# The final norms of a decoder layer: two blocks in one chain, a last accumulation in halves, stores of a quarter megabyte

## The reference

```python
x = _layernorm(x + _L0_ffn_ref(x, gate_weight, gate_up_proj, down_proj, layer_alpha))
# _layernorm: (x - mean) / sqrt(var + 1e-5) over the 256 features
# expert_step, 32 times: h = silu(x @ Wg.T) * (x @ Wu.T); acc += (h @ Wd.T) * c_e[:, None]
```

## Time and profile before

| | |
|---|---|
| device time, 3 runs | 897.95, 898.0, 899.88 us, median 898.0 |
| the profiled execution | 901.3 us, its span 899.5 us, so 1.8 us lie around the span |
| busy: PE, DVE, ACT, POOL | 848.8, 635.6, 281.1, 126.5 us |
| chain that ended last | PE 83%, DVE 11%, issue 3%, ACT 2% |
| last 39.5 us (from 860): PE, DVE, ACT, POOL busy | 26.9, 27.4, 13.0, 7.8 us |
| last instruction of an engine ends, end of the span | 896.4, 899.5 us |

### The profile page before, as it was taken

How to read it: one execution, slowest core, us unless ns; L and a number is a source line. 1 busy time by engine, 2 the same in 40 slices (tenths; PEclk the granted TensorE clock), 3 DMA queues, 4 the chain that set the end, 5 groups by cost and what they waited for, 6 DMA issues and landing times.

```text
span 899.5 us, 14653 instructions
## 1 busy us (share of the span) xinstructions
PE 848.8 (94%) x5696; PEld 668.4 (74%) x5696; DVE 635.6 (71%) x1390; ACT 281.1 (31%) x502; POOL 126.5 (14%) x101
## 2 busy tenths in 40 slices
PE   5999999999999999999797999999999999999994
PEld 4967677776777768776566788888888888888873
DVE  3565787878878888779687866656665666666557
ACT  4521153112432124211354423233332323232232
POOL 2014400343013330134122100000000000000021
PEclk9999999999999999999998999999999999999997
DMA  9210000100001000000310041020302020000001
GB/s 346 107 36 2 1 2 1 32 17 17 1 1 48 1 16 1 0 25 4 128 58 24 1 140 52 22 65 1 111 23 65 0 86 36 23 1 1 1 23 71
DMA packets 12686, 35.84 MB, mean 40 GB/s; under 512 B 1488, under 2 KB 2384, under 8 KB 12112
## 3 DMA queue, kind: packets, MB, share of 16 engines
q1 hardware_dynamic: 12624, 34.98, 11.1%
HBM read 30.33 MB, written 2.36 MB: 36 GB/s over the span
## 4 chain that ended last, share of the span: by engine, by line
PE 83%; DVE 11%; issue 3%; ACT 2%; DMA 0%; POOL 0%; ACTq 0%; DVEq 0%
PE ps L243 21%; PE ps L244 20%; PE ps L245 20%; PE ps L1398 6%; PE ps L1478 4%; PE ps L1469 2%; PE ps L1280 2%; PE ps L1454 1%; PE ps L1316 1%; PE ps L1234 1%; DVE small L255 1%; DVE small L1079 1%; PE ps L1445 1%; PE ps L1345 1%; DVE stats L923 1%
## 5 line engine op out<-in xcount | busy, mean ns | idle before, releaser
L500 DVE TENSOR_TENSOR su<-sg,ps 128x512 f32<-128x512 f32 x96 | 66.0, 688 | 134.4 <-PE ps L245 133.2
L243 PE MATMUL ps<-y_hi,f_hi 128*128 128x512 f32 x384 | 150.6, 392 | 0.0
L244 PE MATMUL ps<-y_lo,f_hi 128*128 128x512 f32 x384 | 150.1, 391 | 0.0
L245 PE MATMUL ps<-y_hi,f_lo 128*128 128x512 f32 x384 | 150.1, 391 | 0.0
L370 ACT ACTIVATE sg<-ps 128x512 f32<-128x512 f32 x96 | 57.4, 598 | 264.4 <-PE ps L245 264.4
L723 POOL TENSOR_TENSOR roped<-prod 128x512 f32<-128x512 f32 x64 | 81.0, 1288 | 175.3 <-DVE prod L1024 175.3
L1024 DVE TENSOR_TENSOR prod<-ps,ropeq 128x512 f32<-128x512 f32 x128 | 79.3, 681 | 27.9 <-PE ps L245 27.3
L245 PEld LDWEIGHTS ps<-y_hi,f_lo 128*128 128x128 f32 x384 | 72.5, 189 | 15.3
L243 PEld LDWEIGHTS ps<-y_hi,f_hi 128*128 128x128 f32 x384 | 72.5, 189 | 14.9
L244 PEld LDWEIGHTS ps<-y_lo,f_hi 128*128 128x128 f32 x384 | 72.4, 189 | 15.0
L243 PE MATMUL ps<-xT_hi,a_hi 128*128 128x512 f32 x192 | 78.8, 410 | 2.1 <-DVE xT_lo L949 2.1
(11 more groups left out here) (157 smaller groups left out, 1369.5 us busy)
## 6 DMA issues: line engine op xcount, KB each, us to landing
cb<-routing SPq DMA_DIRECT2D x32, 256.0 KB
f_raw<-in_L_ffn_gate_up_proj SPq DMA_DIRECT2D x8, 768.0 KB, 5.2
f_raw<-in_L_ffn_down_proj SPq DMA_DIRECT2D x8, 384.0 KB, 5.8
xb<-in_x SPq DMA_DIRECT2D x4, 512.0 KB, 4.2
lq<-in_L_xattn_Wq SPq DMA_DIRECT2D x1, 2048.0 KB, 14.4
x2T_all<-in_L_xattn_Wo SPq DMA_DIRECT2D x1, 2048.0 KB, 8.3
x2T_all<-x2T SPq DMA_DIRECT2D x4, 512.0 KB, 3.2
out<-res SPq DMA_DIRECT2D x4, 512.0 KB, 2.6
```

What stands on the lines that cost most here:

```text
L243: pe.matmul(dst, l_hi, r_hi, start=first, stop=False, skip_group_check=check)
L244: pe.matmul(dst, l_hi, r_lo, start=False, stop=False, skip_group_check=check)
L245: return pe.matmul(dst, l_lo, r_hi, start=False, stop=last, skip_group_check=check)
L500: dve.tensor_tensor(su[:, k % 2], sg[:, k % 2], bank(2 * (k % 2) + 1), ALU.mult).then_inc(s_su, 1)
```

## The change

The ends of blocks 0 and 1 are placed by tables, one for each part: turn_out at the end of steps 17 and 20, stats at the end of steps 18 and 21, scale at the end of steps 19 and 22, and apply at the head of steps 20 and 23, ahead of the Silu. Accumulate(7) is two instructions, one for each half of the features; turn_out takes the features' half as its outer loop, and for block 3 the second half alone waits for the second instruction. Stats(2) and stats(3) are followed by one scale chain over 8 columns (8 bn_aggr, then the 12 tiny instructions on 128x8). Of blocks 2 and 3 VectorE applies tiles 0 and 1, ScalarE tiles 2 and 3. Their results leave in four stores of 256 KB, one for each pair of tiles.

```diff
-    FINAL_STEP = 18
+    TURN_OUT_STEPS, STATS_STEPS, SCALE_STEPS, APPLY_STEPS = (17, 20), (18, 21), (19, 22), (20, 23)
 # ScalarE
             for k in range(STEPS):
+                if last and k in APPLY_STEPS:
+                    final_apply(APPLY_STEPS.index(k))
                 act.wait_ge(s_g, base + k + 1)
 ...
-                if last and k == FINAL_STEP + 3:
-                    final_apply(0)
             if last:
                 hi(STEPS - 1)
-                final_apply(1)
                 final_apply(2)
                 final_apply(3)
         def final_apply(n):
-            act.wait_ge(s_scale, n + 1)
-            for t in range(2 if n == LAST else TILES):
+            act.wait_ge(s_scale, min(n, LAST - 1) + 1)
+            for t in range(0 if n < LAST - 1 else 2, TILES):
 # SyncE
+        for n in range(LAST - 1):
+            sp.wait_ge(s_res, TILES * (n + 1))
             sp.dma_start(out[n], res[:, n]).then_inc(s_out, 16)
+        for n in (LAST - 1, LAST):
+            sp.wait_ge(s_res_end, 2 * (n - LAST + 2))
+            sp.dma_start(out[n, :, 0:2], res[:, n, 0:2]).then_inc(s_out, 16)
+            sp.wait_ge(s_res, TILES * (LAST - 1) + 2 * (n - LAST + 2))
+            sp.dma_start(out[n, :, 2:4], res[:, n, 2:4]).then_inc(s_out, 16)
 # VectorE
+        def final_stats(n):
+            y = final_sum(n)
+            own.need()
+            for t in range(TILES):
+                dve.wait_ge(s_ft, n + 1 + (t // 2 if n == LAST else 0))
+                own.step(dve.bn_stats(fst[:, TILES * n + t, :], y[:, t]))
+        def final_scale(n, blocks):
+            i = slice(TILES * n, TILES * (n + blocks))
 ...
-                dve.tensor_tensor(acc[:, :, cols(n)], acc[:, :, cols(n)], ps[:, 6:8, :], ALU.add).then_inc(s_acc, 1)
+                for m in (slice(0, KC),) if nb < NB - 1 or not last else (slice(0, 1), slice(1, 2)):
+                    dve.tensor_tensor(acc[:, m, cols(n)], acc[:, m, cols(n)], ps[:, 6 + m.start:6 + m.stop, :], ALU.add)\
+                        .then_inc(s_acc, 1)
 ...
+                if last and k in STATS_STEPS:
+                    final_stats(STATS_STEPS.index(k))
+                if last and k in SCALE_STEPS:
+                    final_scale(SCALE_STEPS.index(k), 1)
             if last:
-                final_norm(1, 1)
-                final_norm(2, 0)
+                final_stats(LAST - 1)
                 accumulate(NB - 1)
-                final_norm(2, 1)
-                final_norm(3, 0)
-                final_norm(3, 1)
+                final_stats(LAST)
+                final_scale(LAST - 1, 2)
 ...
 # TensorE, turn_out and its places
+                for m in range(KC):
+                    if n == LAST and m == 1:
+                        pe.wait_ge(s_acc, GROUPS * BLOCKS + 2)
+                    for t in range(TILES):
 ...
-                if last and k == FINAL_STEP:
-                    turn_out(0)
-                if last and k == FINAL_STEP + 3:
-                    turn_out(1)
+                if last and k in TURN_OUT_STEPS:
+                    turn_out(TURN_OUT_STEPS.index(k))
```

More of the change, by code:

```diff
@@ L147, in build @@
     res = sb(ffn, "res", [P, BLOCKS, TILES, D])
[L148 to L152, removed]
+    fst = sb(ffn, "fst", [P, BLOCKS * TILES, 6])
+    fmv = sb(ffn, "fmv", [P, BLOCKS * TILES, 2])
+    fnt = sb(ffn, "fnt", [P, 2, BLOCKS * TILES])
+    fscale = sb(ffn, "fscale", [P, 2, BLOCKS * TILES])
     ffn.close()
@@ L403, in final_apply @@
             y = final_sum(n)
-            act.wait_ge(s_scale, n + 1)
-            for t in range(2 if n == LAST else TILES):
-                act.activation(res[:, n, t], y[:, t], ACT.Identity, bias=fscale[:, n, 1, t:t + 1],
-                               scale=fscale[:, n, 0, t:t + 1]).then_inc(s_res, 1)
+            act.wait_ge(s_scale, min(n, LAST - 1) + 1)
+            for t in range(0 if n < LAST - 1 else 2, TILES):
+                i = TILES * n + t
+                act.activation(res[:, n, t], y[:, t], ACT.Identity, bias=fscale[:, 1, i:i + 1],
+                               scale=fscale[:, 0, i:i + 1]).then_inc(s_res, 1)
         over_groups(act, body)
@@ L450, in ffn_sync @@
                     load_c(w, 2 * it + w + 2, n)
[L451 to L454, removed]
+        for n in range(LAST - 1):
+            sp.wait_ge(s_res, TILES * (n + 1))
             sp.dma_start(out[n], res[:, n]).then_inc(s_out, 16)
-        sp.wait_ge(s_out, 16 * BLOCKS)
+        for n in (LAST - 1, LAST):
[3 more added lines that the diff above has]
+            sp.dma_start(out[n, :, 2:4], res[:, n, 2:4]).then_inc(s_out, 16)
@@ L458, in ffn_vector @@
+        sp.wait_ge(s_out, 16 * (BLOCKS + 2))
     def ffn_vector(dve, own, shift_logits, route):
         dve.sem_inc(s_acc, 1)
-        def final_norm(n, part):
+        def final_stats(n):
             y = final_sum(n)
             own.need()
[L465 to L478, removed]
+            for t in range(TILES):
+                dve.wait_ge(s_ft, n + 1 + (t // 2 if n == LAST else 0))
+                own.step(dve.bn_stats(fst[:, TILES * n + t, :], y[:, t]))
@@ new lines, in final_scale @@
+        def final_scale(n, blocks):
+            i = slice(TILES * n, TILES * (n + blocks))
+            own.need()
+            for t in range(i.start, i.stop):
+                own.step(dve.bn_aggr(fmv[:, t, :], fst[:, t, :]))
+            own.need()
+            own.step(dve.tensor_scalar(fnt[:, 0, i], fmv[:, i, 1], LN_EPS, None, ALU.add))
+            rsqrt(dve, own, fnt[:, 0, i], fscale[:, 0, i], fnt[:, 1, i])
+            own.need()
+            dve.scalar_tensor_tensor(out=fscale[:, 1, i], in0=fmv[:, i, 0], scalar=-1.0, in1=fscale[:, 0, i],
+                                     op0=ALU.mult, op1=ALU.mult).then_inc(s_scale, 1)
+            dve.wait_ge(s_scale, n + 1)
@@ L516, in body @@
                     route(LAST, ROUTE_STEPS.index(k))
[L517 to L520, removed]
+                if last and k in STATS_STEPS:
+                    final_stats(STATS_STEPS.index(k))
+                if last and k in SCALE_STEPS:
+                    final_scale(SCALE_STEPS.index(k), 1)
             if last:
-                final_norm(1, 1)
-                final_norm(2, 0)
+                final_stats(LAST - 1)
                 accumulate(NB - 1)
-                final_norm(2, 1)
-                final_norm(3, 0)
-                final_norm(3, 1)
[L528 to L531, removed]
+                final_stats(LAST)
+                final_scale(LAST - 1, 2)
+                for n in (LAST - 1, LAST):
+                    y = final_sum(n)
+                    for t in (0, 1):
+                        i = TILES * n + t
+                        dve.tensor_scalar(res[:, n, t], y[:, t], fmv[:, i, 0:1], fscale[:, 0, i:i + 1],
+                                          ALU.subtract, ALU.mult).then_inc(s_res_end, 1)
         over_groups(dve, body)
@@ L579, in turn_out @@
                 f = FINAL_BANKS[n]
-                for t in range(TILES):
-                    for m in range(KC):
+                for m in range(KC):
+                    if n == LAST and m == 1:
+                        pe.wait_ge(s_acc, GROUPS * BLOCKS + 2)
+                    for t in range(TILES):
                         c = n * BT + t * P
@@ L584, in turn_out @@
                                           acc[:, m, c:c + P], ident[:])
-                mm.then_inc(s_ft, 1)
+                        if m == KC - 1 and (t == TILES - 1 or n == LAST and t == 1):
+                            mm.then_inc(s_ft, 1)
             for k in range(STEPS):
```

## The result

The changed kernel is slower: median 902.68 us of 21 runs (900.51 to 904.21) against 899.73 of 21 runs of the kernel before on the same chips. The ratio is 1.0036 (95% interval 1.0026 to 1.0046), that is 3.2 us (2.3 to 4.1). Forecast were 3.6, put on 898.0, the median of three runs: 901.6. The median of the 21 runs before is 1.7 higher than that, which is why 902.68 lies above 901.6 although the change cost less than forecast. The profiled execution has a span of 902.2 us, before 899.5.

What follows compares the result with a forecast made beforehand. TensorE was taken to bound the kernel until the last steps, VectorE the end behind dn(23). Later end including stores 2.8 plus clock 0.8 gave 3.6 us slower, 901.6 us on the median 898.0; range 899.2 to 904.0.

Steps and rivals of the forecast that it cites:

- The clock: TensorE's clock around dn(22) and dn(23), after two waits of 1.8 us: may fall; 0.8 us taken, bounds 0 and 2.7.
- Accumulate(5) behind scale(0): Step 20: accumulate(5) and dn(18) 1.44 us later, turn_out(1)'s 0.68 wait gone; TensorE 0.76 later from up(22).
- Accumulate(6): Step 23: scale(1) ahead of it makes it 2.20 us later; TensorE waits 1.8 us before dn(21).
- Apply(1) ahead of Silu(23): Step 23, ScalarE: holds Silu(23), Copy(22), rest(22); second TensorE wait 1.8 us, dn(22) 4.0 later, dn(23) 4.3 later.
- The tail: Behind dn(23): from the last dn on the end is 1.7 us shorter; last apply 2.6 later than before.
- the rival with columns priced one by one: Shared scale chain: tiny instructions on 8 columns cost 12 x 0.16 = 1.9 us more, 903.5; chance 0.03.
- The stores: End of the kernel: a megabyte leaves in about a microsecond; last landing 2.4 to 3.0 us later, 2.8 taken.
- the first rival, the clock that holds: Clock holds or bytes are quick: only 2.4 to 3.0 us slower, 900.4 to 901.0; chance 0.2.
- The rival *faster: Silu(23) and Copy(22) not held: only step 20's 0.76 reaches dn(23), the shorter end wins, 897.1; chance 0.09.

Runs made afterwards that it cites:

- apply_behind: Changed kernel with apply(0) and apply(1) at the end of steps 20 and 23, behind Silu and Copy; ratio 1.0059 to the kernel before.
- apply1_last: Changed kernel with apply(1) moved behind the loop, apply(0) still ahead of Silu(20); ratio 1.0027 to the kernel before.
- loop_only: Kernel before with only the change's placement of turn_out, stats, scale and apply, old tail kept; ratio 1.0039 to the kernel before.
- block2_early: one_more_step with turn_out(2) between up(23) and dn(21), block 2's own scale chain ahead of accumulate(7), block 2 stored whole; ratio 0.9947 to the kernel before.
- loop_back: Changed kernel with blocks 0 and 1 placed as in the kernel before, new tail kept; ratio 0.9998 to the kernel before.
- one_more_step: Changed kernel with stats at the end of steps 17 and 20, scale 18 and 21, apply 19 and 23 behind Silu and Copy; ratio 0.9969 to the kernel before.
- acc_whole: Changed kernel with accumulate(7) as one 128x1024 instruction, all 8 transposes behind it; ratio 1.0038 to the kernel before.

## Why the prediction was right

The mechanism held point by point. The clock's term didn't, and two errors of the end cancelled.

- *Accumulate(5) behind scale(0)*: its start was predicted at 866.48 and is found at 866.56, dn(18)'s second matmul at 868.13 and 868.24. Turn_out(1) has no wait, as said, and up(22) is 0.8 us later than before (0.76 predicted).
- *Accumulate(6)*: predicted at 881.62 and found at 881.65; dn(21)'s second matmul at 883.27 and 883.33.
- *Apply(1) ahead of Silu(23)*: the Silu was predicted at 883.57 and is found at 883.47, rest(22) is ready at 885.93 (predicted 886.06). TensorE's second wait is there and ends with it, hc(23) is 1.6 us long under GpSimd, and dn(23)'s second matmul is at 888.89 (predicted 889.03).
- *The tail*: predicted 1.7 us shorter from the last dn to the last apply's end, found 10.78 - 8.79 = 2.0. Stats(3) begin 2.3 us behind the last matmul's start where 2.5 were estimated, and the longer chain costs less: 8 bn_aggr take 0.64 us where four took 0.37, 0.27 more and not 0.4. The 12 tiny instructions take 0.17 each on 8 columns, against 0.16 on 4, so the rival with columns priced one by one falls.
- *The stores*: the sum gives them 2.8 - 2.6 = 0.2 us more than before; they take 0.5 more (3.6 against 3.1 us behind the last apply). This hides the 0.3 of the tail: without the clock the span's end was forecast at 899.5 + 2.8 = 902.3 and is found at 902.2. That part is luck.
- *The clock*: 0.8 us were put in for it, and in the profiled execution it is nothing. What happened is the first rival, the clock that holds, which had a chance of 0.2 and a price of 2.4 to 3.0 us. The sum without the clock, 2.8, is what the traces differ by, 2.7. The stretch from 482.4 us, from which the fall was argued, doesn't carry over: in the changed kernel TensorE is busy for 1.75 us between 881.2 and 885.9, and the granted clock is 1.00 there and behind it. Apply_behind has a fall behind one wait of 2.75 us and none behind another, apply1_last has none behind a third. What decides it, no run here shows.
- *The timed runs* differ by 3.2 (2.3 to 4.1), nearer to the forecast than the traces are. Executions lie in three groups (last section), and group against group the medians differ by 2.5 to 2.8. The rest is that 9 of the 21 runs of the changed kernel lie in the slowest group and 3 in the fastest, where the kernel before has 6 and 8. Whether the change does that or chance, isn't shown; so that 3.6 came out close is in part luck too.

The rival *faster* had a premise wrong that no term of the prediction looks at: with Silu(23) not held, not only the 0.76 of step 20 would be left. The rest comes earlier too, and runs into the scale chain. Apply1_last has the last dn still 3.3 us later than before (37.94 against 34.65).

The step that carried the forecast was to read the order of instructions on VectorE and ScalarE together, and to ask for each moved piece what stands behind it in its queue. "Moved up by one step" sounds like more slack. It was less: the scale chain had stood behind an accumulate and came to stand in front of it, and an apply had stood behind a Silu and came to stand in front of it.

## What to carry to other kernels

On engines that run strictly in order, a piece moved to an earlier step is late work for everything that it now stands in front of; what counts is not the step but whether the next instruction on this engine is one that the bounding engine waits for. One step up cost 0.4% (loop_only); one more step up, with one step's work between chain and accumulate and the applies behind the Silu, won 0.3% together with the new tail. A tail in which one engine works alone is shortened best by starting its pieces as soon as their inputs exist (block2_early), and a merged chain that saves 1.8 us gives most of it back if it also gathers the last applies and stores at the end.

## What was not expected of the hardware

*A tiny VectorE instruction of the scale chain, all operands in SBUF, that starts while a GpSimd instruction runs is held until that ends.* It was read from one row before (1.14 us); apply_behind, apply1_last, loop_back and one_more_step have it again, each with an end within 0.03 us of GpSimd's. For hc, 128x512, about 0.55 us follow behind GpSimd's end. Not held are su and the bn_stats, which read PSUM, and one that reads SBUF alone: in block2_early, where GpSimd works from 879.93 to 881.22, the four bn_aggr take their usual 0.38 us, and the instruction behind them 0.27 instead of 0.17, to 881.24:

```profile
880.56 0.38 DVE L476 BATCH_NORM_AGGREGATE fmv<-fst 128x2 f32<-128x6 f32 x4
880.97 0.27 DVE L478 TENSOR_SCALAR fnt<-fmv 128x4 f32<-128x4 f32 x1
```

The Trainium skill (SBUF — State Buffer, SBUF: two separate sides) states an exclusive lock on a shared pair of ports between GpSimd and a VectorE instruction that has two SBUF inputs or runs in a 2-port mode; the held rows with two SBUF inputs agree with it. No run tried the same chain with the rest on another engine.

*Execution times of one kernel lie in groups.* The 21 runs of the changed kernel are 900.5 to 900.9, 901.6 to 902.7 and 903.8 to 904.2, those of the kernel before the same some 2.6 us lower. The granted clock, as a mean over each execution, goes with them: in the 28 runs of the kernel before that were timed beside loop_back it is 0.990 to 0.991 in those of 898.1 to 898.5 us, 0.988 to 0.989 from 899.2 to 900.2, and 0.985 to 0.986 from 901.3 to 901.9. Where it falls is in the traces. Stretches of the profiled executions of before and of loop_back, whose code is the same up to the last body (PEclk is the third number from the end):

```profile
50.00:60.00 10.00, 8.39 (x49) 5.86 (x46) 6.13 (x26) 5.69 (x9) 0.00 (x0) 0.83 0.24 81
484.00:492.00 8.00, 6.53 (x31) 5.62 (x32) 4.10 (x10) 2.78 (x4) 0.00 (x0) 0.79 0.17 66
```

```profile
50.00:60.00 10.00, 7.69 (x49) 5.24 (x46) 5.50 (x24) 4.88 (x9) 0.00 (x0) 1.00 0.24 80
484.00:492.00 8.00, 7.72 (x43) 6.71 (x44) 4.65 (x11) 4.61 (x7) 0.00 (x0) 1.00 0.17 66
```

Between 50 and 60 us and between 484 and 492 the clock was reduced in the one and full in the other, and accumulate(4) starts at 850.98 in the one, at 848.33 in the other. The two stretches don't cost alike: block2_early and loop_only, reduced in the first alone, have accumulate(4) at 848.79 and 848.61, acc_whole, reduced in the second alone, at 849.71. Apply1_last, whose slow execution the end doesn't explain, has a mean clock of 0.57 between 438 and 450 us, against 0.86 in before, and accumulate(4) at 851.14. Falls of the clock ahead of the last body move the whole end of the kernel by as much as the change is worth. That these falls make the groups fits the clocks, and no run tested it; why the clock falls in some executions and not in others is open.
